# Two fused transformer layers on one core: new instruction orders in drain, chunk and tail, and a first stage that routes by maxima

## The reference

```python
xn = layernorm(x)
x = x + deltanet_16_heads(xn) + (routed_8_experts(xn) + shared_mlp(xn))       # layer 0
xn = layernorm(x)
x = x + test_time_training_chunks(xn) + batch_experts(xn)                      # layer 1

def _route(x2d, rw, bias):                       # routing of layer 0: 8 experts in 4 groups of 2
    scores = sigmoid(x2d @ rw.T)
    sfc = scores + bias
    group_scores = sum of the two sfc of a group
    masked = sfc where the token's two best groups are, 0 elsewhere
    topk_idx = top_k(masked, 2)                  # two experts; of equal values the lower index
    topk_w = scores[topk_idx] / (sum + 1e-20) * 2.5

def step(carry, inp):                            # layer 1, one chunk of 64 tokens
    ... gate, hidden and their gradients from w0, w1, w2
    w_i = normed(w_i + newtonschulz5(gradient_i))    # two steps; i = 0, 1, 2
    oi = silu(qi @ w0) * (qi @ w2) @ w1
```

## Time and profile before

| | us |
|---|---|
| runs of the kernel | 1736.66, 1736.71, 1745.48 |
| their median | 1736.71 |
| the profiled execution, its own time | 1745.52 |
| its span in the trace | 1743.7 |
| first stage | 0 to 98.5 |
| experts | 98.5 to 200 |
| attention loop | 200 to 1296 |
| drain | 1296 to 1395 |
| chunk periods | 1395 to 1643 |
| tail | 1643 to 1744 |

### The profile page before, as it was taken

One profiled execution on the slowest core, in us unless ns is written; L12 is line 12 of the kernel. 1 busy time (PEld: TensorE's weight loads), 2 busy tenths in 40 slices (PEclk: granted clock), 3 DMA queues, 4 the chain that ended last, 5 costly groups with the idle time before them and its releaser, 6 DMA issues.

```text
span 1743.7 us, 41662 instructions
## 1 busy us (share of the span) xinstructions
PE 1667.6 (96%) x14070; PEld 1230.2 (71%) x14070; DVE 1467.7 (84%) x3684; ACT 1200.7 (69%) x2911; POOL 1101.3 (63%) x1149
## 2 busy tenths in 40 slices
PE   7999899999999999999999999999997689999989
PEld 5577567777777777777777777777765566777667
DVE  5322599999999999999999999999995799999963
ACT  2134467777777777777777777777763488888863
POOL 1600057777777777776666666666665668888851
PEclk9999999999999999999999999999998899999999
DMA  9433300110101101100001000000001000000023
GB/s 314 155 99 113 107 27 27 35 35 24 34 28 30 37 24 33 34 24 25 22 21 30 15 28 24 18 24 27 15 10 49 13 1 2 2 2 1 2 77 107
DMA packets 66098, 73.85 MB, mean 42 GB/s; under 512 B 10975, under 2 KB 54767, under 8 KB 65775
## 3 DMA queue, kind: packets, MB, share of 16 engines
q1 hardware_dynamic: 62919, 63.92, 12.5%
q0 software_dynamic: 3072, 8.65, 1.5%
HBM read 55.45 MB, written 17.10 MB: 42 GB/s over the span
## 4 chain that ended last, share of the span: by engine, by line
PE 85%; DVE 7%; ACT 4%; POOL 2%; issue 1%; SPq 0%; DMA 0%; DVEq 0%; POOLq 0%
PE banks L735 20%; PE banks L894 7%; PE banks L762 4%; PE banks L770 3%; PE banks L849 3%; PE banks L868 3%; PE banks L778 3%; PE banks L807 3%; PE banks L700 3%; PE banks L815 3%; PE banks L821 2%; PE banks L1029 2%; PE banks L814 2%; PE banks L950 2%; PE banks L719 2%; PE banks L860 2%
## 5 line engine op out<-in xcount | busy, mean ns | idle before, releaser
L735 PE MATMUL banks<-xnT,hw 128*128 128x512 f32 x768 | 414.3, 623 | 2.5 <-DVE cv L2045 2.5
L2101 DVE CAST_PREDICATED MM<-lmask,banks 128x512 bf16<-128x512 uint32 x384 | 272.6, 710 | 40.2 <-PE banks L815 34.2
L2045 DVE SCALAR_TENSOR_TENSOR cv<-banks,hc,cv 128x510 f32<-128x510 f32 (+2 forms) x384 | 284.9, 742 | 5.5 <-ACT cv L1448 0.8
L1512 ACT ACTIVATE T<-banks 128x256 bf16<-128x256 f32 x384 | 148.5, 387 | 156.2 <-PE banks L807 156.2
L2711 POOL TENSOR_TENSOR X<-X,yrow 128x512 f32<-128x512 f32 x128 | 163.2, 1276 | 67.9 <-ACT yrow L1544 67.9
L2675 POOL TENSOR_TENSOR kn<-nsum,half_pos 128x4 f32<-128x4 f32 x64 | 65.5, 1023 | 144.4 <-DVE nsum L2070 144.4
L815 PEld LDWEIGHTS banks<-MM,T 128*128 128x128 bf16 x1536 | 104.2, 98 | 64.4 <-issue 47.6
L814 PEld LDWEIGHTS banks<-T,MM 128*128 128x128 bf16 x1280 | 98.8, 97 | 66.3 <-ACT T L1512 64.7
L807 PEld LDWEIGHTS banks<-MM,Gb 128*128 128x128 bf16 x1536 | 84.2, 98 | 82.8 <-issue 44.4
L2045 DVE SCALAR_TENSOR_TENSOR cv<-banks,hcv,cv 128x510 f32<-128x510 f32 (+2 forms) x192 | 141.4, 736 | 1.4 <-ACT cv L1448 1.3
L894 PE MATMUL banks<-ho,OT 128*128 128x256 f32 x512 | 142.2, 401 | 0.0
(11 more groups left out here) (318 smaller groups left out, 4838.6 us busy)
## 6 DMA issues: line engine op xcount, KB each, us to landing
MM<-in_eye SPq DMA_DIRECT2D x64, 256.0 KB, 2.7
slot_rows<-zeros SPq DMA_DIRECT2D x1, 5304.0 KB, 20.5
xs<-slot_rows SPq DMA_DIRECT2D x13, 408.0 KB, 4.0
slot_out<-ye SPq DMA_DIRECT2D x13, 384.0 KB, 2.7
hw<-in_hw SPq DMA_DIRECT2D x16, 256.0 KB, 3.3
wT<-in_winit SPq DMA_DIRECT2D x8, 384.0 KB, 3.9
wgu<-in_wgu SPq DMA_DIRECT2D x1, 2816.0 KB
w1c<-in_ew SPq DMA_DIRECT2D x16, 176.0 KB
```

The lines of the kernel that those rows point to most:

```text
L735: ins = pe.matmul(PROJ[t][:], hw[:, kk, t, :], xnT[:, kk, u.b * BLK:(u.b + 1) * BLK], start=(kk == 0), stop=(kk == KD - 1))
L1512: act.activation(strips(T1[:].rearrange("p i t -> p (i t)"), LEVELS[lv], 0, 1), grams_bank(u)[:, 0:TILES * 64].rearrange("p (k e) -> p k e ...
L2045: dve.scalar_tensor_tensor(o, y, taps_of(t)[:, TAPS - 1 - i:TAPS - i], o, ALU.mult, ALU.add).then_inc(dve_conv, 1)
L2101: dve.copy_predicated(dst, m, ps).then_inc(dve_mm, 1)
```

## The change

In the first stage:

- SP loads in another order: block 0 of X, `ident`, block 1, `wbr`, `wsg`, `wsu`, blocks 2 and 3, then the other constants and `wsd`. PE no longer waits for all constants ahead of its first instruction.
- PE begins with 11 matmuls of zeros, starts to turn when block 0 is normed, and has the units of gate and up in another order around the logits (units 1 to 3 ahead of the mask's matmul, before it units 0 to 2).
- Two of ACT's and DVE's instructions for unit 0 stand ahead of the sigmoid and the routing.
- The routing finds the best of 8 experts by a maximum, takes it out, and finds the next; ranks by pairs are left for the 4 groups alone. The steps to the mask are 19, not 15, and small ones. Slots are handed to POOL in two halves.
- `shared_down(3)` stands in two halves behind the turns of the first two tiles of the experts.

In drain, chunk and tail the lists of all engines are reordered. In the chunk the period's beginning is moved round (STAGES = 6), so that most of the difference there is where the loop's body starts; a few calls really change places.

```diff
@@ SP
-            for g in range(NBLK):
+            load_tokens(0)
+            sp.dma_start(ident[:], a["ident"]).then_inc(s_out, 16)
+            load_tokens(1)
+            sp.dma_start(wbr[:], a["wbr"]).then_inc(s_out, 16)
+            for dst, src in ((wsg, "wsg"), (wsu, "wsu")):
+                sp.dma_start(dst[:], a[src]).then_inc(moe_w, 16)
+            load_tokens(2)
+            load_tokens(3)
@@ PE
-            pe.wait_ge(s_const, 11 * 16)
+            pe.wait_ge(s_out, 16 * FIRST_CONSTANTS)
+            pe.wait_ge(*s_half)
+            for _ in range(11):
+                pe.matmul(bank[5][:, 0:2 * P], zeros[:, 0:P], zeros[:, 0:2 * P], start=True, stop=True)
             ln_turn(0)
...
-            shared_down(NBLK - 1)
@@ PE, experts
                     turn_x(n)
+                    if n < 2:
+                        shared_down(NBLK - 1, range(n * TPB // 2, (n + 1) * TPB // 2))
@@ DVE, routing
+            def largest(v, chosen):
+                step(dve.tensor_reduce(top, v, AX.X, ALU.max))
+                step(dve.tensor_tensor(found, v, top.unsqueeze(2).to_broadcast([P, NT, E0]), ALU.is_ge))
+                step(dve.scalar_tensor_tensor(found, places, float(NT * P), found, ALU.subtract, ALU.mult))
+                step(dve.tensor_reduce(top, found, AX.X, ALU.min))
+                step(dve.tensor_tensor(chosen, found, top.unsqueeze(2).to_broadcast([P, NT, E0]), ALU.is_equal))
-            ranks(r_mask[:], 8, lt8)
+            largest(r_mask[:], chosen_of[0])
+            step(dve.scalar_tensor_tensor(r_rank[:], chosen_of[0], -3e38, r_mask[:], ALU.mult, ALU.add))
+            largest(r_rank[:], chosen_of[1])
...
-            dve.tensor_copy(slots[:], slotf[:]).then_inc(e_slots, 1)
+                dve.tensor_copy(slots[:, :, k], slotf[:, :, k]).then_inc(e_slots, 1)
+            weights_of(1)
@@ POOL, second half of the sends
+                pool.wait_ge(e_slots, TOP0)
@@ POOL, drain
             root_grads(x0)
+            rate_keys(x1)
             rate_powers(3)
             one_minus(x1)
             rate_hidden(x1)
-            rate_keys(x1)
@@ DVE, chunk period
+                do(weight_scale, u4, 0, 1)
+                do(add_rows, u5)
                 do(sum_weights, u4, 1)
-                do(add_rows, u5)
+                do(grad_gate, u1)
                 do(mix, u4)
-                do(grad_gate, u1)
+                do(mean_output, u4)
                 do(weight_scale, u3, 0, 0)
-                do(mean_output, u4)
-                do(weight_scale, u3, 0, 1)
                 do(newton, u2, 0, 0, NEXT)
+                do(norm_output, u4)
@@ PE, tail (of some 30 places)
-            newton(x12, 1, 1, NEXT)
-            project_v(x15)
-            newton(x13, 0, 1, GRAM)
-            turn_weight(x12, 0)
+            newton(x13, 0, 1, SQUARE)
             total(x14)
-            newton(x13, 0, 1, SQUARE)
...
             up(0)
+            turn_weight(x14, 0)
             newton(x14, 1, 1, SQUARE)
-            newton(x15, 0, 0, NEXT)
+            newton(x15, 0, 1, TURN)
             turn_output(x13)
+            up(1)
```

More of the change, by code:

```diff
@@ L627, in logits, with shared_gate @@
                     last.then_inc(pe_once, 1)
-            ln_turn(0)
[L630 to L633, removed]
-            def shared_up(b):
[L636 to L640, removed]
-                    for kk in range(KD):
[L642 to L646, removed]
+            def shared_gate(n, kk):
+                b, f = divmod(n, FS0)
+                rows = SROWS[f]
+                if n >= 3 and kk == 0:
+                    pe.wait_ge(m_silu, n - 2)
+                ins = pe.matmul(bank[2 * (n % 3)][0:rows], wsg[:, kk, f * P:f * P + rows], xnT[:, kk, b * BLK:(b + 1) * BLK],
+                                start=(kk == 0), stop=(kk == KD - 1))
+                if kk == KD - 1:
+                    ins.then_inc(m_gate, 1)
@@ new lines, in _ @@
+            logits(2)
+            pe.wait_ge(ln_kept0, NBLK + 2)
+            pe.wait_ge(ln_kept1, NBLK + 2)
+            pe.wait_ge(s_const, 10 * 16)
+            logits(3)
+            for kk in range(KD):
+                shared_gate(1, kk)
+            for kk in range(KD):
+                shared_raise(1, kk)
+            for kk in range(KD):
+                shared_gate(2, kk)
+            for kk in range(KD):
+                shared_raise(2, kk)
+            for kk in range(KD):
+                shared_gate(3, kk)
@@ L647, in shared_up @@
+            for kk in range(KD):
+                shared_raise(3, kk)
+            def shared_up(b):
+                for n in range(max(b * FS0, 4), (b + 1) * FS0):
+                    for kk in range(KD):
+                        shared_gate(n, kk)
                     for kk in range(KD):
-                        last = pe.matmul(bank[2 * r + 1][0:rows], wsu[:, kk, f * P:f * P + rows], xnT[:, kk, b * BLK:(b + 1) * BLK],
-                                         start=(kk == 0), stop=(kk == KD - 1))
@@ L655, in shared_down @@
                     pe.wait_ge(e_slots, 1)
-                for t in range(TPB):
+                for t in those:
                     if b and t % 2 == 0:
@@ L1366, in _ @@
             newton(x15, 1, 0, NEXT)
-            down(2)
+            output(x14)
             turn_weight(x15, 0)
             newton(x15, 1, 1, TURN)
-            output(x14)
+            down(2)
+            turn_weight(x15, 1)
+            turn_output(x14)
             newton(x15, 1, 1, GRAM)
@@ L1373, in _ @@
             newton(x15, 1, 1, SQUARE)
-            turn_output(x14)
-            turn_weight(x15, 1)
+            up(4)
             newton(x15, 1, 1, NEXT)
-            up(4)
             gate_queries(x15)
@@ L1380, in _ @@
             up(6)
+            turn_weight(x15, 2)
             turn_mixed(x15)
-            turn_weight(x15, 2)
             down(4)
@@ L2524, in _ @@
             norm_qk(x15, 0)
+            norm_qk(x15, 1)
             sum_grads(x14, 1)
-            norm_qk(x15, 1)
             norm_qk(x15, 2)
```

467 lines of the change are left out of this document (243 added, 224 removed).

## The result

| | us |
|---|---|
| kernel before, 20 runs, median | 1741.28 (1734.92 to 1746.96) |
| changed kernel, 20 runs, median | 1747.53 (1744.52 to 1753.23) |
| ratio | 1.0039, 95% interval 1.0025 to 1.0053 |
| changed kernel's profiled execution | 1747.48, span 1744.8 |

The changed kernel is 0.4% slower: less than the 0.5% that was to count as a change, but clear of noise. One thing has to be known to read the numbers: the times of the kernel before lie in two groups, ten of 20 runs near 1736.6 (1734.92 to 1739.09) and ten near 1745.5 (1743.48 to 1746.96), and the execution profiled ahead of the prediction was of the upper group. So it takes 2 us more than the upper group and 11 more than the lower.

A forecast was written before the change was run, and what follows sets the result against it. PE was taken as the bound, busy 1667.6 of 1743.7 us, with the sends close to it in the first stage. 1745.5 - 2.9 (first stage) + 0 (drain) + 0 (chunk) - 4 (tail) = 1738.6, range 1725 to 1750.

The forecast's parts named there:

- rivals 1 and 4: 1: clock stays low in first stage, 1748.8, chance 0.15; 4: a new list is worse, 1743 to 1749, chance 0.10.
- First stage, -2.9: Start to first expert: 5.0 us earlier, less 2.1 for the clock after idling; bounds -8 and +0.6.
- The zeros: PE's first matmuls: run from about 1.5, end by 6.3 ahead of the rows, cost nothing, may raise the clock.
- The logits: First stage: 1.9 us a block if the clock is up, ending at 26.6, ACT's last copy at 27.2.
- The end: End of first stage: PE idles 4.9 us before xs at 87.9; clock loss 2.1; first expert at 93.6.
- Routing by maxima, worth nothing behind PE's units: First-stage routing: DVE saves some 2.5 us, mask near 34.3, hidden behind PE's units until 37.5.
- The clock behind a wait: First stage: bursts after a transfer wait start at the lower clock; idling before xs costs 2.1 us, bounds 0 and 3.5.
- The row at 1368: Profile window cited as agreeing with the clock rule: granted clock 0.50 after two microseconds without a matmul.
- Drain and chunk, 0 and 0: Reordered lists: no net gain; drain bounds -4 and +3, chunk -1.3 and +4 over 13 periods.
- Tail, -4: Tail: new lists fill part of PE's idle and slow time from 1643 to 1686; bounds -8 and +2.
- I take half: Tail: half of 7.2 us idle and about 1.5 us of clock taken as gained, -4.
- The 8.8 us: Profiled execution's excess over median 1736.71: perhaps first-stage low clock, so faster runs already have the gain; new runs near 1738.6.

The follow-up runs named there:

- a_nozeros: The changed kernel with its loop of 11 matmuls of zeros left out; median 1746.13 us, ratio 1.0039 to the kernel before.
- a_downahead: The changed kernel with the last shared down in one piece ahead of the wait for xs; median 1740.45 us, ratio 1.0014 to the kernel before.
- b_same: The kernel before with no edit, traced a second time; measured 1736.73 us, in the lower group.

## Why the prediction held, and where its steps did not

The forecast (1738.6, range 1725 to 1750, most likely no change by 0.5%) holds the median of 1747.53, by its edge, and that is luck more than insight. Both terms that made its sum had the wrong sign, and both came out beyond their own bounds (+0.6 and +2). The range reached up to 1750 for rivals 1 and 4, neither of which came about as written. And slower was to begin at 1745.4, counted from a median of 1736.71 in which the lower group prevailed; 1747.53 is above it, and the kernel counts as unchanged because 20 runs of before have their median at 1741.28.

- **First stage, -2.9.** Measured +1.3 against the execution that the sum was made from. *The zeros* were put at nothing, done by 6.3. They stand behind PE's wait for the first constants (6.71), and a matmul of them is two records, not one: 22 records took 7.46 us. Yet this held back the first expert by only 0.6 (a_nozeros). *The logits* ran at the full clock, as forecast, but the unit behind them began at 29.2, not 27.2. *The clock then fell* for unit 1, 1.6 us that no term had. Together xs came at 91.3, not 87.9. *The end* was forecast best: 5.0 idle for 4.9, and 2.5 of clock for 2.1. That the halved down loses what it would fill is shown by a_downahead, 7.05 us; it was in the working, and I let the gain ahead of it outweigh it.
- **Routing by maxima, worth nothing behind PE's units.** Right in the changed kernel (mask ready at 36.4, taken at 41.0). From DVE's first step to the mask it is 6.6 us for 10.0 before, a saving of 3.4 where 2.5 was forecast. In the lower group of before DVE's ranks come last, by 0.18 us, so there too the saving could not bring much while three units stand ahead of the mask.
- **The clock behind a wait.** The Trainium skill ("TensorE: Matmul & The Clock Gate", section "HAM oscillation — how this bites in real kernels") says that a burst behind a wait for a transfer starts at the lower clock. The half down behind xs bears it out: 5.28 for 2.76, at a granted clock of 0.50 after 5.0 us of idle time. What rival 1 drew from it for the logits was wrong: they ran at 1.86 a block with and without zeros. And the fall at 28 us had no such wait ahead of it. The row at 1368 that the forecast names stands behind 3.0 us in which PE waited for DVE, not for a transfer, so it shows the lower clock behind idle time as such.
- **Drain and chunk, 0 and 0.** Right, as far as the traces can tell.
- **Tail, -4.** Measured +2.2, and the same length in six kernels. The step that failed is "I take half": idle time of PE was taken for something that a new order would fill, without following one list against what DVE had to do in it. From 1643 to 1686 PE idles 8.5 us, not under 4, where it idled 7.2.
- **The 8.8 us.** The forecast took the lower group of times for executions with the full clock in the first stage. b_same shows that, to 8.4 us. It also said that the gain in the first stage is then one that those runs already have. Right, and too mild: the new kernel is 9.8 later at its first expert than b_same, 3.0 by later sends and 6.7 behind xs.

No rival came true as it stood; the nearest is the fourth, a list that is worse.

## What to carry to other kernels

Work that is ready belongs ahead of a wait, not behind it: behind it costs its own length, and the clock's fall as well. When a kernel's times lie in two groups, take a trace of each before costing a change, since a gain against one can be something that the other already has. Idle time in a profile is no gain until the new list has been followed step by step on the engine that PE waits for.

## What was not expected of the hardware

The same program showed two courses from 15 us on, 1.90 or 3.24 us for the same 16 records, and the profile's windows print PEclk 1.00 for both, so durations are what to read there. With the new first stage the granted clock fell at 28 us in eight of ten traces, to 0.50, and not in two, under a PE that was never idle. And in one batch every kernel, the one before too, took 16 to 20 us more; where traces were taken, PE got its matmuls between 66 and 92 us singly, with up to 2.5 us of idle time between them and no engine or transfer named. Its cause is open.
